# A hybrid layer on one core: the block-sparse layers' softmax by halves, their bias by matmul, the last one inside the mixer's block

## What is computed

```python
dots = jax.nn.softmax(x @ centroids.T / TEMPERATURE, axis=-1)
hits = dots > THRESHOLD
query_sel = jnp.any(hits, axis=1)
cluster_sel = jnp.any(hits, axis=0)
row_sel = cluster_sel[assignments]
dense = x @ weight.T + bias
out = jnp.where(query_sel[:, None] & row_sel[None, :], dense, jnp.zeros((), dense.dtype))
```

## Time and profile before

| | |
|---|---|
| median of three executions | 1948.48 us |
| the profiled execution | 1951.1 us |
| its span | 1949.4 us |
| PE busy | 1825.2 us (94%) |
| DVE busy | 1349.2 us (69%) |
| ACT busy | 1173.8 us (60%) |
| POOL busy | 1443.3 us (74%) |
| mean granted TensorE clock | 0.969 |

### The profile page before, as it was taken

One profiled execution on the slowest core, in us unless ns is written; L12 is line 12 of the kernel. 1 busy time (PEld: TensorE's weight loads), 2 busy tenths in 40 slices (PEclk: granted clock), 3 DMA queues, 4 the chain that ended last, 5 costly groups with the idle time before them and its releaser, 6 DMA issues. The chain is left out here.

```text
span 1949.4 us, 32318 instructions
## 1 busy us (share of the span) xinstructions
PE 1825.2 (94%) x10772; PEld 1456.6 (75%) x10772; DVE 1349.2 (69%) x1717; ACT 1173.8 (60%) x2120; POOL 1443.3 (74%) x1430
## 2 busy tenths in 40 slices
PE   6998997688999999999999999999999999999967
PEld 4765775467887888788878878887888788878845
DVE  5654564666766776686768767776776786768756
ACT  3222333358675776677677767675776677577723
POOL 4312323538996999799879978996999799879854
PEclk9997997889999999999999999999999999999978
DMA  3000001112222232132222322222232132222201
GB/s 109 1 2 23 1 2 33 33 60 98 93 90 73 77 98 100 60 98 76 88 77 92 98 67 92 82 92 73 76 104 97 56 98 76 87 76 92 76 27 49
DMA packets 107398, 136.66 MB, mean 70 GB/s; under 512 B 9040, under 2 KB 74704, under 8 KB 107216
## 3 DMA queue, kind: packets, MB, share of 16 engines
q1 hardware_dynamic: 106256, 134.28, 20.8%
q10 hardware_dynamic: 960, 0.05, 0.0%
HBM read 131.67 MB, written 2.62 MB: 69 GB/s over the span
## 5 line engine op out<-in xcount | busy, mean ns | idle before, releaser
L144 PE MATMUL ps<-mix_xnT_hi,mix_w_hi 128*128 128x512 f32 x1152 | 461.7, 401 | 6.8 <-DVE mix_bT L1580 6.8
L146 PE MATMUL ps<-mix_xnT_hi,mix_w_lo 128*128 128x512 f32 x1152 | 455.3, 395 | 0.0
L145 PE MATMUL ps<-mix_xnT_lo,mix_w_hi 128*128 128x512 f32 x1152 | 455.2, 395 | 0.0
L1580 DVE SCALAR_TENSOR_TENSOR mix_xT<-ps,mix_cur,mix_xT 128x510 f32<-128x510 f32 x378 | 279.9, 745 | 143.9 <-ACT mix_xT L1402 134.9
L1333 POOL TENSOR_SCALAR_AFFINE_SELECT mix_spread<-mix_spread 128x256 f32<-128x256 f32 x512 | 320.4, 660 | 0.0
L1600 DVE TENSOR_TENSOR mix_decay<-mix_decay,mix_cb 128x1536 f32<-128x1536 f32 x128 | 291.1, 2312 | 4.5 <-ACT mix_decay L1428 4.5
L1451 ACT ACTIVATE mix_g_hi<-mix_gated 128x512 fp32r<-128x512 f32 x128 | 81.0, 633 | 315.0 <-POOL mix_gated L1310 283.6
L144 PEld LDWEIGHTS ps<-mix_xnT_hi,mix_w_hi 128*128 128x128 f32 x1152 | 217.6, 189 | 56.4 <-issue 8.4
L146 PEld LDWEIGHTS ps<-mix_xnT_hi,mix_w_lo 128*128 128x128 f32 x1152 | 217.5, 189 | 50.9
L1426 ACT ACTIVATE mix_decay<-mix_spread,mix_cur_ncum 128x256 f32<-128x256 f32 x512 | 253.7, 496 | 1.6 <-issue 1.6
L145 PEld LDWEIGHTS ps<-mix_xnT_lo,mix_w_hi 128*128 128x128 f32 x1152 | 217.8, 189 | 47.6
(11 more groups left out here) (254 smaller groups left out, 3416.7 us busy)
## 6 DMA issues: line engine op xcount, KB each, us to landing
mix_spread<-cum_rows SPq DMA_DIRECT2D x128, 512.0 KB, 4.0
mix_w_raw<-in_w_in_stream SPq DMA_DIRECT2D x144, 256.0 KB, 4.1
mix_wo_raw<-in_w_out_T SPq DMA_DIRECT2D x64, 256.0 KB, 3.4
att_w_raw<-in_w_attn_T SPq DMA_DIRECT2D x12, 256.0 KB, 4.0
x<-in_x SPq DMA_DIRECT2D x8, 256.0 KB, 4.3
ffn_w_raw<-in_w_ffn_T SPq DMA_DIRECT2D x2, 1024.0 KB, 5.8
out_rows<-x SPq DMA_DIRECT2D x8, 256.0 KB, 2.0
att_wp_raw<-in_w_proj_T SPq DMA_DIRECT2D x4, 256.0 KB, 2.8
```

The source lines that it names most:

```text
L144: pe.matmul(out, lh, rh, start=(k == 0), stop=False)
L145: pe.matmul(out, lh, rl, start=False, stop=False)
L146: last = pe.matmul(out, ll, rh, start=False, stop=(k == tiles - 1))
L1580: dve.scalar_tensor_tensor(out=d[:, :, shift:T], in0=src[:, :, 0:T - shift], scalar=w[:, MK - 1 - shift:MK - shift], in1=d[:, :, shift:T], ...
```

## The change

The block-sparse layer is split into parts (`ffn_parts`) that both of its uses call.

- **Softmax by halves.** Logits, their copy, their transpose, and all DVE steps up to the row's hit run for tiles 0 to 3 and then for tiles 4 to 7. On PE the order after the turns becomes: logits of half 1, dense `done`, turn logits 1, turn best 0, dense `done`+1, 6 matmuls of the next dense, turn best 1, the rest of it, the mask, and the other dense products. `done` is 0 in ffn1 and 2 in ffn2.
- **Bias by matmul.** Each dense product gets a 13th matmul, of two rows of ones with the high and the low part of the bias. DVE's mask times bias, ACT's 8 masked biases and POOL's 8 additions go. DVE masks each dense product; the addition to x is POOL's for even tiles and DVE's for odd ones.
- **In ffn1**, POOL makes the bias parts (a copy, a subtraction, two selects, an addition on 2 partitions of 512) between the small operations of tiles 3 to 7, and the one-hot matrix of the assignments, which was DVE's. Centroid parts, one-hot matrix and bias parts are kept for the second use.
- **ffn2 in the mixer's block.** The barrier between them goes. Its weights are loaded at k = 4 of the last group into the space of B and C, and split by ACT and POOL at k = 7, ahead of `high` and of `gate_pair`. `row_of_x` on DVE takes an out row, adds a tile to x and lets its statistics follow at once. On PE the last two out rows and the halves of dense 0 and dense 1 stand between the turns.
- **Gate's products.** At k = 0 of every group the two halves of ("g", 1) stand after C times B of batches 0 and 1 and after that of batches 2 and 3, and DVE copies batches 2 and 3 after both halves of the convolution. In the last group, ("g", 7) is made at k = 7 and not at k = 6.

The core of the diff:

```diff
+def ffn_parts(nc, sh, ctx, tag, m, ln, logit_banks, dense_banks):
...
+    def dense_rows(pe, t, before_dense, first=0, end=STEPS):
+        if first == 0:
+            if t == 0:
+                pe.wait_ge(f.w_lo_done, KT)
+                before_dense()
+            pe.wait_ge(ln.s["lo"], t + 1)
+            at_least(pe, dense_read, t - len(dense_banks) + 1)
+        bank, rows = ps[:, dense_banks[t % len(dense_banks)], :], ln.place(t)
+        for n in range(first, end):
+            if n == 0:
+                last = pe.matmul(bank, sh.two_ones[:, :], sh.bias_parts[:, :], start=True, stop=False)
+            else:
+                k, kind = (n - 1) // 3, (n - 1) % 3
+                last = pe.matmul(bank, (ln.lo if kind == 2 else ln.hi)[:, k, rows],
+                                 (m.w_lo if kind == 1 else m.w_hi)[:, k, :], start=False, stop=(n == STEPS - 1))
+        if end == STEPS:
+            last.then_inc(dense, 1)
...
+    def turn_best(pe, h):
+        pe.wait_ge(sm, SOFT * h + 6)
+        pe.transpose(ps[0:NCL, ln.bank0, h * P:(h + 1) * P], m.best[:, h, :], sh.ident[:, :]).then_inc(best_T, 1)
+    def spread_mask(pe):
+        pe.wait_ge(sm, LAST)
+        pe.matmul(ps[:, ln.bank0 + 1, :], m.chosen, sh.one_hot[:, :], start=True, stop=True).then_inc(mask_ps, 1)
...
+    def wait_x(engine, t):
+        engine.wait_ge(f.x_odd if t % 2 else f.x_even, t // 2 + 1)
+    def add_part(engine, t):
+        engine.wait_ge(dense_read, t + 1)
+        engine.tensor_tensor(x[:, t, :], x[:, t, :], m.part[:, t % 4, :], ALU.add)\
+              .then_inc(f.x_odd if t % 2 else f.x_even, 1)
...
+    def best_half(dve, h):
+        rows, prob = half_of(h), m.prob[:, half_of(h), :]
+        dve.wait_ge(ex, h + 1)
+        dve.tensor_reduce(m.row[:, 1, rows], prob, AX.X, ALU.add).then_inc(sm, 1)
+        dve.wait_ge(sm, SOFT * h + 3)
+        dve.reciprocal(m.row[:, 2, rows], m.row[:, 1, rows]).then_inc(sm, 1)
+        dve.wait_ge(sm, SOFT * h + 4)
+        dve.tensor_tensor(prob, prob, m.row[:, 2, rows].unsqueeze(2).broadcast_to([P, 4, NCL]), ALU.mult)\
+           .then_inc(sm, 1)
+        dve.wait_ge(sm, SOFT * h + 5)
+        dve.tensor_reduce(m.best[:, h, :], prob.rearrange("p t c -> p c t"), AX.X, ALU.max).then_inc(sm, 1)
+        dve.tensor_reduce(m.row[:, 0, rows], prob, AX.X, ALU.max).then_inc(sm, 1)
+        dve.wait_ge(sm, SOFT * h + 7)
+        dve.tensor_scalar(m.row[:, 3, rows], m.row[:, 0, rows], THRESHOLD, None, ALU.is_gt).then_inc(sm, 1)
...
+    def cluster_mask(dve):
...
+        dve.wait_ge(mask_ps, 1)
+        dve.tensor_copy(m.mask, ps[:, ln.bank0 + 1, :]).then_inc(masked, 1)
+        dve.wait_ge(masked, 1)
+    def take_dense(dve, t):
+        dve.wait_ge(dense, t + 1)
+        if t >= 4:
+            wait_x(dve, t - 4)
+        dve.scalar_tensor_tensor(out=m.part[:, t % 4, :], in0=ps[:, dense_banks[t % len(dense_banks)], :],
+                                 scalar=m.row[:, 3, t:t + 1], in1=m.mask, op0=ALU.mult, op1=ALU.mult)\
+           .then_inc(dense_read, 1)
+    def rows_pool(pool):
+        for t in range(0, NT, 2):
+            add_part(pool, t)
...
+    def rows_pe(pe, between, done, before_logits, before_dense, before_mask):
+        def dense(t, first=0, end=STEPS):
+            dense_rows(pe, t, before_dense, first, end)
+        for t in range(NT):
+            ln.turn_pe(pe, t)
+            if t == 5:
+                before_logits()
+                half_logits(pe, 0)
+            between(t, dense)
+            if t == 6:
+                turn_logits(pe, 0)
+        half_logits(pe, 1)
+        dense(done)
+        turn_logits(pe, 1)
+        turn_best(pe, 0)
+        dense(done + 1)
+        dense(done + 2, 0, 6)
+        turn_best(pe, 1)
+        dense(done + 2, 6)
+        before_mask()
+        spread_mask(pe)
+        for t in range(done + 3, NT):
+            dense(t)
...
+    def rows_dve(dve, row_of_x, before_mask):
+        for t in range(3):
...
+            if t + 3 < NT:
+                row_of_x(t + 3)
+                ln.stats_dve(dve, t + 3)
+            ln.lo_dve(dve, t)
+        centre_half(dve, 0)
+        best_half(dve, 0)
+        centre_half(dve, 1)
+        best_half(dve, 1)
+        before_mask()
+        cluster_mask(dve)
+        for t in range(NT):
+            take_dense(dve, t)
+            if t % 2:
+                add_part(dve, t)
...
+    def rows_act(act, between):
+        ln.normalize_act(act, 0)
+        for t in range(NT):
+            if t + 1 < NT:
+                ln.normalize_act(act, t + 1)
+            ln.hi_act(act, t)
+            between(t)
+            if t == 6:
+                copy_logits(act, 0)
+        exp_half(act, 0)
+        copy_logits(act, 1)
+        exp_half(act, 1)
...
             pool.iota(cluster_id[:, :], pattern=[[0, 1]], base=0, channel_multiplier=1,
                       allow_small_or_imprecise_dtypes=True).then_inc(made, 1)
+            pool.memset(two_ones[:, :], 1.0).then_inc(bias_done, 1)
+            pool.wait_ge(bias_done, 1)
+            pool.tensor_copy(sh.two_ones[:, :], two_ones[:, :]).then_inc(bias_done, 1)
             for t in range(4):
...
-                pool.wait_ge(bias_hit_ready, t + 1)
-                pool.tensor_tensor(x[:, t, :], x[:, t, :], bias_hit[:, t % 2, :], ALU.add).then_inc(summed, 1)
+            pool.wait_ge(bias_in, 16)
+            pool.tensor_copy(bias_high[:, :], bias[:, :]).then_inc(bias_done, 1)
+            ln.rstd_pool(pool, 4)
+            pool.wait_ge(bias_done, 3)
+            pool.tensor_tensor(bias_low[:, :], bias[:, :], bias_high[:, :].bitcast(F32), ALU.subtract)\
+                .then_inc(bias_done, 1)
+            pool.wait_ge(bias_done, 4)
+            pool.affine_select(out=bias[:, :], in_=bias_high[:, :].bitcast(F32), compare_op=ALU.is_ge, fill=0.0,
+                               base=0, pattern=[[0, C]], channel_multiplier=-1).then_inc(bias_done, 1)
+            ln.rstd_pool(pool, 5)
+            pool.affine_select(out=bias_low[:, :], in_=bias_low[:, :], compare_op=ALU.is_ge, fill=0.0,
+                               base=-1, pattern=[[0, C]], channel_multiplier=1).then_inc(bias_done, 1)
+            pool.wait_ge(bias_done, 6)
+            pool.tensor_tensor(sh.bias_parts[:, :], bias[:, :], bias_low[:, :], ALU.add).then_inc(bias_done, 1)
+            ln.rstd_pool(pool, 6)
+            f.w_low(pool, 0)
+            ln.rstd_pool(pool, 7)
+            for k in range(1, KT):
+                f.w_low(pool, k)
+            pool.wait_ge(misc, 16)
+            pool.wait_ge(made, 2)
...
+        m.part = flat(gated[:, :, :], "s t").rearrange("p (s c) -> p s c", c=C)
+        ln = build_layernorm(nc, sh, ctx, "ffn2_ln", 0, into=(xnT_hi, xnT_lo),
+                             xn=square[:, :].rearrange("p (s c) -> p s c", c=C))
...
+        def gate_in(last, k):
+            if last and k >= PAIRS - 2:
+                return PAIRS - 1 if k == PAIRS - 1 else None
+            return k + 1
...
+                    if last and k == 4:
+                        sp.wait_ge(aux, n_aux(g, ("cb", B - 1)) + 1)
+                        sp.dma_start(m.w_raw, ins["w_ffn_T"].rearrange("(k p) n -> p k n", p=P)).then_inc(f.w_in, 16)
...
                         pool.wait_ge(spread_in[1], 16 * (PAIRS * g + k + 2))
+                    else:
+                        pool.wait_ge(projected, 2 * (N_PRODUCTS - 1))
+                        for j in range(KT):
+                            f.w_low(pool, j)
                     gate_pair(g, k)
...
             group_rstd(MG - 1, TAIL + 4 + 2)
+            for t in range(NT):
+                ln.rstd_pool(pool, t)
+            f.rows_pool(pool)
...
+                    gate = gate_in(last, k)
+                    if gate:
                         if not (first and k == 0):
-                            act.wait_ge(squared, PAIRS * g + k)
-                            act.wait_ge(g_lo_done, 2 * (PAIRS * g + k))
-                        silu_gate(n_product(g, ("g", k + 1)), gated[:, buf, :])
+                            act.wait_ge(squared, PAIRS * g + gate - 1)
+                            act.wait_ge(g_lo_done, 2 * (PAIRS * g + gate - 1))
+                        silu_gate(n_product(g, ("g", gate)), gated[:, gate % 2, :])
                     if k < PAIRS - 1:
                         load_exp()
+                    if not has_next:
+                        act.wait_ge(aux, n_aux(g, ("out", k, 3)) + 1)
+                        for j in range(KT):
+                            f.w_high(act, j)
                     high(g, k, first)
...
             square_pair(MG - 1, PAIRS - 1, False)
+            load_exp()
+            act.wait_ge(summed, (PAIRS - 1) * MG)
+            f.rows_act(act, lambda t: None)
...
-                        take_cb(g, (2, 3))
                     if k == 1 and not first:
                         variance(n_aux(g, ("var", 0)))
                     if has_next:
```

(49 more changed lines are left out.)

286 lines of the change are left out of this document (128 added, 158 removed).

## The result

| | before | after |
|---|---|---|
| median | 1944.2 us | 1941.67 us |
| lowest to highest | 1941.36 to 1951.77 (20 runs) | 1935.89 to 1948.33 (20 runs) |
| ratio, 95% interval | | 0.9978 (0.9968 to 0.9989) |
| profiled execution, its span | 1951.1, 1949.4 | 1942.55, 1940.7 |

The account below looks back on a forecast made before the run. PE bounds the mixer (1257 of 1274 us busy), the order of steps bounds the block-sparse layers and the mixer's end. -12.3 - 1.0 - 10.3 + 0.4 = -23.2 gave a median of 1925 us; forecast 1921 to 1930, wider range 1918 to 1936.

Parts of the forecast that it names:

- Part 1: Gate's products at k = 0 of each group: PE's 1.76 us wait goes, 7 x 1.76, -12.3 us; bounds 0 to 13.3.
- the first group: Group 0 of the mixer: y waits for mix there and DVE's sum up to mix is the same, so 0.
- PE has no other wait behind this ... so each gain is carried on: Mixer groups: no further PE wait until the last pair, so each 1.76 us counts in full, 12.3 us.
- Mix becomes the wait: Rival, 12 in 100: y waits for mix at k = 0, margin 0.6 us; part 1 gives 0 to 4 us, 1933 to 1937.
- Not later: Mixer at k = 0: the other engines, with ACT's silu and POOL's next split, are freed earlier, not later; no cost given.
- Part 2: Last pair: ("g", 7) fills PE's idle time, POOL's low parts delay the gate; -1.0 us, bounds -2.0 and +3.4.
- Part 3: Mixer's end and ffn2: barrier gone, softmax by halves, shorter chain after the mask; -10.3 us, bounds -13 and -4.
- the 13th matmul costs a full step: Dense products of the block-sparse layers: the 2-row bias matmul costs one step like the others, 13 x 0.228 = 2.96 us.
- the rival on the clock: Rival, 13 in 100: turns hold PE at 1.2 GHz from 1889 to 1905 in the mixer's end; +3 to +7 us, 1928 to 1932.
- The 1.2 us for out row 6: Mixer's end: out row 6's six matmuls may run at 1.2 GHz, 0.2 us more each; 1.2 us put against the gain.
- Part 4: ffn1: POOL's bias work and the 13th matmul offset the softmax by halves and shorter end; +0.4 us, bounds -3 and +5.
- It would be wrong if a new wait appeared in k = 1 to 7: Sign of failure in each mixer group: any 1 us there counts eight times or fifty-six.

Follow-up runs that it names:

- e1: The kernel before with only the gate's products moved at k = 0 (and the copies of batches 2 and 3); 1932.3 us, ratio to before 0.9940.
- e15: The kernel before, nothing of the change, with 12 transposes more on PE at the start of the first block-sparse layer; 1957.1 us, ratio to before 1.0069.
- e6: e5 with POOL's four low parts of the block-sparse weights behind the last pair's gate; 1924.5 us, ratio to before 0.9890.
- e9: e5 with POOL's four low parts of the block-sparse weights behind the last sum of squares too; 1925.4 us, ratio to before 0.9883.
- e2: The changed kernel with 12 transposes more on PE at the start of the first block-sparse layer; 1931.7 us, ratio to before 0.9920.
- e3: The changed kernel with the bias's matmul on 128 rows (126 zero) in place of 2; 1937.9 us, ratio to before 0.9959.
- e4: The changed kernel with POOL's split of the next weights at k = 0 waiting until mix is done; 1936.5 us, ratio to before 0.9950.
- e8: The changed kernel with 6 transposes more on PE at the start of the first block-sparse layer; 1952.8 us, ratio to before 1.0033.
- e5: The changed kernel with e2, e3 and e4 together; 1923.8 us, ratio to before 0.9883.
- e13: The changed kernel with 128 transposes (256 instructions) more on PE at the start of the first block-sparse layer; 1949.3 us, one run.
- e14: The changed kernel with 10 transposes more on PE at the start of the first block-sparse layer; 1932.6 us, one run.
- e12: e9 with the product of the last gate, ("g", 7), back at k = 6; 1924.2 us, ratio to before 0.9885.
- e10: e9 with the first half of the logits turned behind turn 7 of the layernorm; 1922.9 us, ratio to before 0.9885.
- e7: e1 with 11 transposes more on PE at the start of the first block-sparse layer; 1947.2 us, ratio to before 1.0005.
- e11: e9 with all eight final additions to x in both block-sparse layers on DVE, none on POOL; 1923.7 us, ratio to before 0.9885.

## Why the prediction was wrong

**What bounds the kernel**: right. PE is full in the mixer before and after, and the order of the steps sets the time of the layers.

**Part 1, -12.3**: right as a part, wrong in this kernel. In e1 the period falls by 2.1 in each group, more than 1.76, since y follows sooner too, and L by 11.1. One term was given as 0 and isn't: the first group. PE waits for mix there in any case, 2.9 to 3.4 us, and in 14 of the 15 kernels with the moved product the period from the first group to the next is 178 us, where it is 175.7 before and 175.9 in e15. The windows of 30 us from its first copy of mix_cb on, before and after:

```profile
441.28:471.28 30.00, 24.49 (x144) 19.76 (x144) 21.27 (x25) 25.20 (x50) 24.02 (x25) 1.00 0.34 113
```
```profile
439.07:469.07 30.00, 25.18 (x124) 19.69 (x122) 20.62 (x24) 22.95 (x47) 22.24 (x21) 0.89 0.28 90
```

The granted clock is 1.00 in the first and 0.89 in the second: the y behind the wait runs at the lower level (its first products take 1.13 and not 0.66 us), and 2.3 us are lost. That it is the order that brings this about I haven't shown: the wait is longest in e6 and e9, 3.40 us, with the high clock in one and the low in the other. In e6, the one kernel that has the product moved and 175.9 us, the clock stayed at 1.00.

The step that failed is "PE has no other wait behind this ... so each gain is carried on". The stall of 6.7 us was not a row of before, and the prediction had no term for what a shift of PE's program does; of the rivals none was it. "Mix becomes the wait", at 12 in 100, did come, 0.86 us in each group, and its margin of 0.6 us was about right. But the condition was not DVE's sum, which the prediction checked, but which POOL operation runs beside mix, which it did not. "Not later" for POOL was true and beside the point: the split came earlier, and onto mix.

**Part 2, -1.0**: -1.5 measured from pair 5's y, and that was luck in this execution. The move makes PE wait 2.2 us ahead of pair 6's y, which before it did not, and the stretch from there to the last y differs between executions of the same work. The wait in after, and then the stretch in after and in e2:

```profile
1845.29 0.66 PE L1984 MATMUL ps<-mix_decay,mix_x_dt 128*64 128x256 f32 x4 [2.20 <-issue]
```
```profile
1845.30:1861.20 15.90, 15.27 (x90) 12.25 (x90) 9.30 (x11) 11.99 (x27) 12.55 (x13) 1.00 0.00 0
```
```profile
1837.60:1855.10 17.50, 16.92 (x88) 13.18 (x88) 9.24 (x11) 11.92 (x27) 12.54 (x13) 0.90 0.00 0
```

The granted clock was 1.00 in five of the twelve kernels with this wait and 0.90 in seven, which is 1.4 to 1.7 us longer. With the last pair as in after, it had the -1.5 in after, e3, e4 and e8, and nothing in e2, e5, e13 and e14. The prediction had no term for it. Its bound of -2.0, with POOL's parts out of the way, was 2.2 in e9 against e12, though e9 had the low clock there. POOL's parts took 4.96 us for the 5.3 that I had. (The bound of +3.4 took 1.1 us for what POOL work beside mix costs; in before most low parts of wo_lo beside mix take 2.8 us for 1.3, so it is 1.5.)

**Part 3, -10.3**: from the first take, before needs 68.9 us and after 63.8, so -5.1. The sequence is as forecast; the terms were too small. Forecast, from the first take and with the 1.2 us put against it: last low part done at 34.7, mask at 48.6, end at 58.6. After has 36.2, 52.7 and 63.8. The 5.2 us are: the bias's matmul 2.0 (e3); six matmuls of the second logits at 0.43 for 0.23, 1.2; the row from mask to end 10.4 in e3 for 10.0, as an addition of DVE beside POOL's takes 1.23 and not 0.95, 0.4; and the last low part 1.3 later (0.2 of its 1.5 are in e3's 2.0), behind the stretch at 0.66. Some 0.2 is left. The first two are the failed step "the 13th matmul costs a full step" and a part of the rival on the clock. That rival put the low clock on the turns from 1889 to 1905; it came in out row 6, half of out row 7 and the two turns between, and again behind PE's wait ahead of the second logits. The 1.2 us for out row 6 were in the forecast; the rest, at 0.43 for 0.23 us a step, cost some 2 us in after, not 3 to 7. In e10, at 0.98 to 1.00 throughout, the row from the first take to the end is 4.5 us shorter than in e9 (the later turning is in it too), so the rival's price was no exaggeration.

**Part 4, +0.4**: +2.9 measured. With the bias on full rows (e3) it is +0.3. So everything else in that sum, POOL's small operations on 2 partitions above all, was sized about right, and the one failed term is the 2-row matmul. (The sum has a slip: 346.0 and 27.8 are 373.8, not 374.2, so its terms give 0.0 and not +0.4.) "512 columns are streamed for 2 rows as for 128" had no row to rest on; it was argued and should have had a bound.

**The sum.** From the first copy of mix_cb to the first take of a last out row, before needs 1436.1 us and after 1434.4. Less part 2's 1.5, the -12.3 of part 1 came to -0.2: by e1 the move is worth 15.3 (2.1 in six groups, 2.7 in the last), and 14.4 went again (stall 6.7, y's wait for mix 8.3 for 2.9, first group 2.3), which would leave -0.9 and not -0.2, so 0.7 is open. With 12.1 missing here, 5.2 in part 3 and 2.5 in part 4, and 0.5 more than forecast in part 2, -23.2 becomes -3.9; L fell by 4.2. The range was too narrow on the slow side, for it held bounds for each part but nothing for a cost that is the program's and not a part's. "It would be wrong if a new wait appeared in k = 1 to 7" looked for it in the wrong place; it came at the jump.

## What to carry to other kernels

Where a kernel loops in hardware, look at PE's idle times without releaser behind the jump in every profile, and try a few instructions more in front of the loop before judging any edit by its time: here that alone was worth more than the edit, in both directions. Where DVE and POOL work from SBUF side by side and one runs at a time, look at what stands between two operations of the one that is waited for: a short one costs it little, a long one its whole length. Give a small matmul in a row of full ones its own measured price, or fill it up. Where a change puts a new wait of 2 us in front of a full stretch of PE, look at the granted clock behind it in more than one execution.

## What the runs showed of the hardware that I had not expected

- A stall of 1.0 to 3.2 us at each jump back of a loop, set by where the loop begins in PE's program, which comes back when 256 instructions are put in front (e2, e4, e7, e8, e13, e15).
- A matmul of 2 rows between those of 128 costs 0.63 us with the steps into and out of it, one of 128 rows 0.23 (e3).
- Of mix or an addition on DVE and a select, split or addition on POOL one runs at a time, and the second to start ends late: mix 3.54 us alone, in groups 1 to 6 of e1 3.63 to 3.89 with selects and in those of after 4.39 with the split beside it; four selects 1.49 alone, 4.56 beside mix; the split 1.04 and 1.28 alone, 1.90 and 2.67 beside mix; an addition of DVE 0.69 alone, 1.23 begun behind POOL's, which stays at 1.28 (after, e1, e4, e11).
- On POOL 2 partitions cost the same as 128: the subtraction of the bias's parts took 1.26 us, that of a weight part 1.28.
- The same order of work has a granted clock of 0.66 in one execution and 1.00 in another over the same ten microseconds (e9, e10), some 2 us of difference; behind the same wait of 2.2 us it was 1.00 in five kernels and 0.90 in seven; and the unchanged attention part ended between 313 and 323 us.
